# One fused VectorE step for the first batch's convolution in a hybrid attention, feed-forward and S4D layer

## What is computed

```python
x = x + _L0_attn_a_ref(_layernorm(x, axis=-1), ...)
x = x + _L0_ffn_ref(_layernorm(x, axis=-1), ...)
x = x + _L0_attn_b_ref(_layernorm(x, axis=-1), ...)   # S4D
x = x + _L0_ffn_ref(_layernorm(x, axis=-1), ...)

# _L0_ffn_ref
gate = jax.nn.silu(_quantized_matmul(x, gate_w, gate_scale))
up = _quantized_matmul(x, up_w, up_scale)
return _quantized_matmul(gate * up, down_w, down_scale)
```

## Time and profile before

| | us |
|---|---|
| median of 3 runs | 141.35 (141.25 to 142.14) |
| span of the profiled execution | 140.5 |
| PE busy | 118.3 (84%) |
| DVE busy | 105.1 (75%) |
| POOL busy | 100.1 (71%) |
| ACT busy | 62.3 (44%) |

### The profile page before, as it was taken

The page is one execution under the profiler, slowest core; times in us unless marked ns, Lnnn a source line. Parts: engine busy times, 40 slices in busy tenths (PEclk is TensorE's granted clock), DMA queues, the critical chain, the costliest instruction groups (busy, mean ns, idle before and its releaser), DMA issues.

```text
span 140.5 us, 2050 instructions
## 1 busy us (share of the span) xinstructions
PE 118.3 (84%) x650; PEld 78.2 (56%) x650; DVE 105.1 (75%) x244; ACT 62.3 (44%) x117; POOL 100.1 (71%) x156
## 2 busy tenths in 40 slices
PE   5489999999999700899999999794999896999950
PEld 5466587585877400785456844453745465446640
DVE  0459999998885896059735699999999998656272
ACT  3124156532331103644795437394454474374500
POOL 6282899998899998997864175669879883029621
PEclk9968999999999995559999999999999999999996
DMA  3999700000000020000000000000000000001304
GB/s 129 281 320 361 225 3 7 2 0 0 0 1 0 0 71 4 7 0 0 0 0 0 0 0 0 2 0 0 0 0 0 0 0 5 0 0 40 109 0 149
DMA packets 5599, 6.03 MB, mean 43 GB/s; under 512 B 900, under 2 KB 4952, under 8 KB 5592
## 3 DMA queue, kind: packets, MB, share of 16 engines
q1 hardware_dynamic: 5464, 5.91, 12.8%
q0 software_dynamic: 128, 0.03, 0.1%
HBM read 4.89 MB, written 1.05 MB: 42 GB/s over the span
## 4 chain that ended last, share of the span: by engine, by line
PE 29%; DVE 29%; POOL 25%; issue 6%; ACT 4%; DMA 3%; SPq 1%; POOLq 0%; DVEq 0%; ACTq 0%
PE psum L1064 15%; PE psum L1077 7%; POOL s4d L304 5%; DVE stats L594 4%; PE psum L1002 3%; DMA x_in<-in_x 3%; DVE fused L843 3%; DVE scaled_down L791 3%; POOL rstd L280 3%; DVE h_rows L832 3%; PE psum L1025 2%; POOL gate L390 2%; POOL up L390 2%; POOL gate_raw L386 2%; POOL up_raw L386 2%
## 5 line engine op out<-in xcount | busy, mean ns | idle before, releaser
L408 POOL TENSOR_TENSOR f_tail<-fused,f_head 128x512 f16<-128x512 f32 x12 | 14.6, 1219 | 15.2 <-ACT f_head L560 15.2
L549 ACT ACTIVATE gated<-psum,scales 128x512 f32<-128x512 f32 x24 | 16.3, 681 | 15.0 <-PE psum L1064 15.0
L1077 PE MATMUL psum<-down,f_head 128*128 128x256 bf16 x96 | 22.0, 273 | 0.1
L1077 PE MATMUL psum<-down,f_tail 128*128 128x256 bf16 x96 | 22.0, 273 | 0.0
L843 DVE SCALAR_TENSOR_TENSOR fused<-psum,up_scales_fit,gated 128x512 f32<-128x512 f32 x24 | 17.5, 738 | 4.7 <-PE psum L1064 3.0
L560 ACT ACTIVATE f_head<-fused 128x512 f16<-128x512 f32 x24 | 15.0, 626 | 10.7 <-DVE fused L843 10.5
L1064 PE MATMUL psum<-h_head,up 128*128 128x512 f16 x48 | 14.3, 379 | 1.3 <-DVE fused L843 1.3
L850 DVE TENSOR_TENSOR f_tail<-fused,f_head 128x512 f16<-128x512 f32 x12 | 9.7, 809 | 7.1 <-ACT f_head L560 7.1
L1064 PE MATMUL psum<-h_tail,up 128*128 128x512 f16 x48 | 14.3, 379 | 0.0
L1064 PE MATMUL psum<-h_head,gate 128*128 128x512 f16 x48 | 14.3, 379 | 0.0
L1064 PE MATMUL psum<-h_tail,gate 128*128 128x512 f16 x48 | 14.3, 379 | 0.0
(11 more groups left out here) (168 smaller groups left out, 267.9 us busy)
## 6 DMA issues: line engine op xcount, KB each, us to landing
x_in<-in_x SPq DMA_DIRECT2D x4, 256.0 KB, 4.4
out<-x_in SPq DMA_DIRECT2D x4, 256.0 KB, 2.1
qkv_sb<-in_qkv SPq DMA_DIRECT2D x3, 256.0 KB, 3.9
gate_raw<-in_gate_w SPq DMA_DIRECT2D x1, 768.0 KB, 6.8
up_raw<-in_up_w SPq DMA_DIRECT2D x1, 768.0 KB, 8.6
down_raw<-in_down_w SPq DMA_DIRECT2D x1, 768.0 KB, 10.3
wo_sb<-in_o_proj SPq DMA_DIRECT2D x1, 256.0 KB, 5.1
taps_all<-taps_dram SPq DMA_DIRECT2D x1, 256.0 KB, 3.0
```

What stands on the lines that cost most here:

```text
L408: pool.tensor_tensor(f_tail[:, m, :], fused[:, m % FUSED, :], f_head[:, m, :], ALU.subtract).then_inc(f_tail_by_pool, 1)
L549: act.activation(gated[:, m % 2, :], psum[:, BANK_GATE[m % 2], :], ACT.Silu, scale=gate_scales[:, m:m + 1]).then_inc(gated_ready, 1)
L1077: last = pe.matmul(column(BANK_DOWN[t // 2], H * (t % 2), H), part[:, m, t * P:t * P + P], down16[:, m, :], start=(m == 0 and t % 2 == 0 a ...
```

## The change

For the first batch, x3 is written as mean + (tap0 + std) * z, since x2 = mean + std * z. VectorE makes (tap0 + std) * z in one step from the z that ScalarE makes for the lagged term anyway, and leaves the mean out. The LayerNorm that follows doesn't see a constant per row; the mean is added in place by ScalarE in pass 2, before the last residual reads x3. GpSimd makes std = var_eps * rstd, one more short step in `inverse_std` behind a wait for rstd. ScalarE's z steps move from behind `f_head` of m = 2 to two pairs, behind `f_head` of m = 0 and of m = 1. The lagged product gets a buffer of its own, since z is now read by two engines. The second batch is computed as before.

```diff
@@ inverse_std (GpSimd)
                 power.then_inc(rstd_ready[n], count)
+                if n == 2 and k < T:
+                    pool.wait_ge(rstd_ready[n], k + count)
+                    pool.tensor_tensor(std2[:, k:k + count], var_eps[:, n, k:k + count], rstd[:, n, k:k + count],
+                                       ALU.mult).then_inc(std_ready, count)
@@ residual (GpSimd)
                 for k in tiles:
+                    if n == 1 and k < T:
+                        pool.wait_ge(x3_whole, k + 1)
@@ lag_tap, add_lag (GpSimd)
-                    mark(pool.tensor_tensor(x_lag[:, t, :], x_lag[:, t, :], taps_all[:, 1, :], ALU.mult))
+                    mark(pool.tensor_tensor(lag_product[:, t, :], x_lag[:, t, :], taps_all[:, 1, :], ALU.mult))
-                pool.tensor_tensor(x2_lag[:, t, :], x2[:, T + t, :], x_lag[:, t, :], ALU.add).then_inc(lag_ready, 1)
+                pool.tensor_tensor(x2_lag[:, t, :], x2[:, T + t, :], lag_product[:, t, :], ALU.add).then_inc(lag_ready, 1)
@@ ScalarE, behind f_head of chunk m
-                    if n == 1 and m == 2:
-                        for t in range(T):
+                    if n == 1 and m in (0, 1):
+                        for t in (2 * m, 2 * m + 1):
                             act.wait_ge(shift_ready[2], t + 1)
                             act.activation(x_lag[:, t, :], x2[:, t, :], ACT.Identity, scale=rstd[:, 2, t:t + 1],
                                            bias=neg_mean_rstd[:, 2, t:t + 1]).then_inc(z2_ready, 1)
+                    if n == 2 and m in (0, 1):
+                        for t in (2 * m, 2 * m + 1):
+                            act.activation(x3[:, t, :], x3[:, t, :], ACT.Identity,
+                                           bias=mean_var[:, 2, t, 0:1]).then_inc(x3_whole, 1)
@@ VectorE
+            def s4d_first(tiles):
+                dve.wait_ge(taps_loaded, 16)
+                for k in tiles:
+                    dve.wait_ge(std_ready, k + 1)
+                    dve.wait_ge(z2_ready, k + 1)
+                    dve.scalar_tensor_tensor(out=x3[:, k, :], in0=taps_all[:, 0, :], scalar=std2[:, k:k + 1],
+                                             in1=x_lag[:, k, :], op0=ALU.add, op1=ALU.mult).then_inc(x3_ready, 1)
@@ VectorE, pass loop
                     tail(n, 0)
-                    s4d_begin(first)
-                    s4d_end(first)
+                    if n == 1:
+                        s4d_first(first)
+                    else:
+                        s4d_begin(first)
+                        s4d_end(first)
                     fuse(n, 2)
                     x3_stats(first)
-                    s4d_begin(second)
+                    if n == 1:
+                        s4d_first(second)
+                    else:
+                        s4d_begin(second)
                     fuse(n, 3)
-                    s4d_end(second)
+                    if n == 2:
+                        s4d_end(second)
```

More of the change, by code:

```diff
@@ L137, in hybrid_layer @@
         x_lag = sb("x_lag", [P, T, H])
+        lag_product = sb("lag_product", [P, T, H])
+        std2 = sb("std2", [P, T])
         x2_lag = sb("x2_lag", [P, T, H])
@@ L157, in hybrid_layer @@
         shift_ready = [None] + [sem(f"shift_ready{n}") for n in (1, 2, 3)]
-        z2_ready = sem("z2_ready")
+        z2_ready, std_ready, x3_whole = sem("z2_ready"), sem("std_ready"), sem("x3_whole")
         z_ready, z_turned = sem("z_ready"), sem("z_turned")
@@ L822, in s4d_end @@
                     dve.wait_ge(rstd_ready[2], k + 1)
-                    if b:
-                        dve.wait_ge(lag_ready, t + 1)
+                    dve.wait_ge(lag_ready, t + 1)
                     dve.scalar_tensor_tensor(out=x3[:, k, :], in0=normed[:, k, :], scalar=rstd[:, 2, k:k + 1],
-                                             in1=x2_lag[:, t, :] if b else x2[:, k, :], op0=ALU.mult,
+                                             in1=x2_lag[:, t, :], op0=ALU.mult,
                                              op1=ALU.add).then_inc(x3_ready, 1)
```

## The result

The changed kernel takes 142.44 us (median of 20 runs, 141.8 to 142.95), the kernel before 141.56 us in its 20 (141.0 to 142.23): a ratio of 1.0063, with a 95% interval of 1.0048 to 1.0077, thus 0.68 to 1.09 us slower.

What follows compares the result with a forecast made beforehand. The end of pass 1 was taken to be set by ScalarE's f_head of chunk 3, through GpSimd's in-order list. 0.96 us there and nothing in passes 2 and 3 gave 141.35 + 0.96 = 142.3 us, range 141.2 to 143.5.

Steps and rivals of the forecast that it cites:

- The pass that is edited and the chain in it: Pass 1: its end, set by f_head of chunk 3 through GpSimd's list, comes 0.96 us later.
- z of tiles 0 and 1, std 0.33: Pass 1, GpSimd and ScalarE: std delays the first neg_mean_rstd by 0.33 us to 85.86; z runs 85.93 to 87.01.
- f_tail of chunk 1 and the second inverse_std: Pass 1, GpSimd: f_tail starts at 88.18 behind the delayed f_head; the inverse_std behind it ends at 91.30, 1.31 us late.
- `f_head` of chunk 3: Pass 1, ScalarE: ends at 94.66 instead of 93.70, +0.96 us, as gated of chunk 3 and f_head of chunk 2 come first.
- Statistics hidden, `norm_rows` in the old order at 2.0 us: End of pass 1, VectorE: statistics end 0.5 us ahead of GpSimd's f_tail; norm_rows again start behind f_tail, taking 2.00 us.
- Pass 2 at nothing: Pass 2, ScalarE: four mean additions, 2.0 us, push gated of chunk 3 but hide in 2.41 us of idle time: 0.
- Rival A: Pass 1: delay absorbed, std steps free and norm_rows ahead of f_tail; -0.1 to +0.3, about 141.4 us; chance 0.13.
- rival B: Pass 1: VectorE's 1.78 us gain reaches norm_rows, 139.6 us, if z of tile 2 starts early enough; chance 0.05.
- Rival C: Pass 1, start of pass 2: TensorE's clock falls after idle gaps, adding 0.4 to 1.7 us: 142.7 to 144.0; chance 0.24.
- The rule on two SBUF inputs: Pass 1, VectorE: by it the new step waits for GpSimd's rstd, x3 of tile 3 0.4 us later; slack covers it.

Runs made afterwards that it cites:

- e2: The changed kernel with GpSimd's std step moved behind neg_mean_rstd in both inverse_std of x2; 141.65 us, ratio 0.9988 to the kernel before.
- e10: The kernel before with the z steps in two pairs and the std steps, VectorE's convolution still in two steps; 143.02 us, ratio 1.0100.
- e1: The changed kernel with GpSimd's second inverse_std of x2 ahead of f_tail of chunk 1 in pass 1; 139.47 us, ratio 0.9839 to before.
- e4: The kernel before with GpSimd's second inverse_std of x2 ahead of f_tail of chunk 1 in pass 1; 141.53 us, ratio 0.9989.
- e3: The kernel before with only ScalarE's z steps moved, in two pairs behind f_head of chunks 0 and 1; 140.97 us, ratio 0.9942.
- e5: The changed kernel without the four ScalarE steps adding the mean in pass 2 and the wait for them; 142.71 us, ratio 1.0074 to before.
- e8: The changed kernel with all four z steps on ScalarE behind f_head of chunk 1; 141.03 us, ratio 0.9939 to the kernel before.
- e9: The kernel before with GpSimd's two std steps and their waits on rstd alone, std read by nobody; 142.27 us, ratio 1.0058.
- e11: The changed kernel with the second inverse_std ahead of f_tail of chunk 1 and std behind neg_mean_rstd; 139.04 us, ratio 0.9815 to before.
- e6: The changed kernel with GpSimd's f_tail of chunk 4 waiting in pass 1 until norm_rows are done; 141.98 us, ratio 1.0027 to before.

## Why the prediction was right

- **The pass that is edited and the chain in it**: right. +0.96 us was worked out for the end of pass 1, +0.87 measured there and +0.88 in the medians. The forecast of 142.3 us lies even nearer to the 142.44 measured, but that is luck: the kernel before was taken at 141.35 us from three runs and is 141.56 in twenty, which made up for the small excess.
- **z of tiles 0 and 1, std 0.33**: neg_mean_rstd was to end at 85.86; it ended at 84.76 + 1.10 = 85.86. e2 and e10 measured 0.65 for both std steps where 0.66 was written.
- **f_tail of chunk 1 and the second inverse_std**: 88.18 and 91.30 forecast, 88.15 and 91.28 measured. e1 and e4 show that it is this order that sets the place of the second inverse_std.
- **`f_head` of chunk 3**: 94.66 forecast, 93.49 + 1.10 = 94.59 measured. The small excess of the forecast is here: ScalarE's four steps took 2.19 us, not 2.22, and z of tile 3 ended 0.04 sooner.
- **Statistics hidden, `norm_rows` in the old order at 2.0 us**: 1.97 us, with `f_tail` 0.06 us ahead of it (95.83 against 95.89). That it was so close is shown by e3 and e10, where it tipped and gave 0.4 us.
- **Pass 2 at nothing**: right, by e5. The size was off: 2.0 us of delay for `gated` of chunk 3, about 1.0 measured. Each pair pushes what follows by 0.80 us instead of 1.0, and about 0.5 us went into idle time that ScalarE had ahead of `f_head` of chunk 1 before. Two additions with only a bias take less than two z steps, which take 1.09 us (timeline of ScalarE in pass 2):

```profile
104.75 0.89 ACT L581 ACTIVATE x_plus<-x_plus,mean_var 128x256 f32<-128x256 f32 x2
...
109.49 0.63 ACT L568 ACTIVATE f_head<-fused 128x512 f16<-128x512 f32 x1 [1.38 <-DVE fused L864]
```

- **Rival A** (absorbed) and **rival B** (faster by 1.78): not so. But the condition that B was tied to proved right. Counted from the start of pass 1 it asked for z of tile 2 before 90.4 - 78.73 = 11.7 us, and for the full gain before 88.6 - 78.73 = 9.9 us. In the changed kernel that step starts 90.21 - 77.63 = 12.6 us into the pass, in e1 87.20 - 77.78 = 9.4, and e1's 139.47 us is near what B would have given (139.6). Between them, e2 starts it at 11.9 us and has pass 1 0.22 us longer than before, e8 at 11.4 us and has it 0.31 shorter: the limit of 11.7 lies between the two.
- **Rival C** (the clock): its event does occur, in the traces of e5 and e10, but its price was wrong. The prediction added 0.4 us or more for it in pass 1. The step "of which `fused` of chunk 5 sees 0.4" was right: VectorE waits 0.62 us for `gated` there instead of 0.24. What failed is that these 0.4 us should reach the end of the pass. `norm_rows` started 0.22 us later (18.48 us into the pass against 18.26) and then spent that much less time beside `f_tail`, 1.74 us instead of 1.97: in both kernels they ended 0.9 us behind the end of that `f_tail`.
- **The rule on two SBUF inputs** (*SBUF — State Buffer*, section Who interferes with whom, of the Trainium skill): the new step of tile 2 ran beside GpSimd's rstd (90.59 to 91.30), and the pair took 0.95 us, waits for z included, against 0.94 for the first pair with GpSimd idle. So VectorE wasn't held by this GpSimd step of 128x2. By `f_tail` it is, and the prediction was right that the new step isn't freed from that: in e8, where the first new step starts beside `f_tail` of chunk 1, one took 891 ns instead of 472.

## What to carry to other kernels

A step moved ahead in one engine's list is paid by what stands behind it there, and then by whatever stands behind the first victim in the next engine's list. Follow it through every in-order list until an engine has slack; here the delay went from ScalarE's list into GpSimd's and came back to ScalarE's, VectorE's and TensorE's. When the change loses that way, look for the exchange in the other list: here a short chain with its input ready stood behind an instruction that waited.

An instruction has no price of its own: adding the same two 0.2 us steps cost 0 us of pass 1 in e9 and 0.65 in e10, and moving them one place back gained 0.65 us in e2 and 0.18 in e11. The whole change cost 0.87 us of pass 1, or gained about 2 with one line moved in another engine's list.

## What the runs showed of the hardware

- VectorE and GpSimd hold each other up, and the order of their starts goes with how long: two `norm_rows` steps take 0.73 us alone (e6), 1.57 when they start 0.14 us ahead of `f_tail` (e3), 1.97 when they start 0.06 behind it (changed kernel). Small GpSimd steps are held too: rstd took 0.98 us in e1 and 1.17 in e11 instead of 0.71, and in e1 mean_rstd took 0.76 us instead of 0.19 beside a VectorE `f_tail`, although its recorded start is 0.02 us ahead (timelines of GpSimd and VectorE):

```profile
89.65 0.76 POOL L290 TENSOR_SCALAR mean_rstd<-mean_var 128x2 f32<-128x2 f32 x1
```

```profile
89.67 0.68 DVE L871 TENSOR_TENSOR f_tail<-fused,f_head 128x512 f16<-128x512 f32 x1
```

- TensorE's granted clock fell to 0.50 after an idle gap of 1.98 us in one execution (e5) and stayed at 1.00 after 1.99 us in another with the same instructions in pass 1 (changed kernel); where it fell, 1.64 us of delay vanished in a later wait.
- SyncE's wait for the last output transfer was 0.6 to 0.9 us longer in three traces (e5, e9, e10) than the 1.8 us of the eleven others. What sets them apart isn't known; no kernel was profiled with both.
